# Lag attention with even and odd output parts, LayerNorm statistics on ScalarE: one change to a four-layer kernel

## The reference, cut to what matters

```python
x = x + tanh(g_xattn[0]) * autocorrelation(layernorm(x), ctx, ctx)      # the lag attention
x = x + tanh(g_ffn[0]) * moe(layernorm(x), ...)                          # its statistics are made in the stage above it

def autocorrelation(Q, K, V):            # K = V = ctx; each column on its own, L = 256 rows
    corr = ifft(fft(q) * conj(fft(k))).real
    w, idx = top_k(corr, 11); w = softmax(w)
    out = sum_i w_i * v[min(idx_i + pos, L - 1)]
```

## Time and profile before

| | |
|---|---|
| median of 3 runs | 1355.69 us (1354.49 to 1355.74) |
| profiled execution | 1356.5 us, of which 1354.8 us from the first to the last instruction (the span) |
| granted TensorE clock, mean | 0.971 |
| busy share of the span | PE 92%, DVE 58%, ACT 38%, POOL 42% |
| lag attention | 0 to 422.6 us: PE 363.6, DVE 341.8, ACT 190.0, POOL 286.9 us busy |
| the three other layers | 422.6 to 1354.8 us |

### The profile page before, as it was taken

One profiled execution on the slowest core, in us unless ns is written; L12 is line 12 of the kernel. 1 busy time (PEld: TensorE's weight loads), 2 busy tenths in 40 slices (PEclk: granted clock), 3 DMA queues, 4 the chain that ended last, 5 costly groups with the idle time before them and its releaser, 6 DMA issues. The chain is left out here.

```text
span 1354.8 us, 20940 instructions
## 1 busy us (share of the span) xinstructions
PE 1239.7 (92%) x6442; PEld 846.7 (62%) x6442; DVE 783.7 (58%) x2026; ACT 513.5 (38%) x939; POOL 573.0 (42%) x931
## 2 busy tenths in 40 slices
PE   4799999999878999999999998999999999968886
PEld 2354544445435954458888786988888898635443
DVE  3889999998963680015433333444554443369885
ACT  2555545454423400023322222232222322168894
POOL 5667877777642001013221222523212231068884
PEclk8999999999988899999999999999999999879998
DMA  5211212302004502227778874535333331131111
GB/s 197 92 64 32 93 62 96 138 31 109 0 1 149 224 1 84 70 85 246 265 240 283 273 233 161 187 94 128 114 103 124 96 101 54 62 70 47 62 62 78
DMA packets 52481, 156.25 MB, mean 115 GB/s; under 512 B 5952, under 2 KB 16192, under 8 KB 52288
## 3 DMA queue, kind: packets, MB, share of 16 engines
q1 hardware_dynamic: 39152, 113.46, 23.6%
q0 software_dynamic: 13264, 41.95, 10.8%
HBM read 112.93 MB, written 45.61 MB: 117 GB/s over the span
## 5 line engine op out<-in xcount | busy, mean ns | idle before, releaser
L1210 PEld LDWEIGHTS ex_bank<-ex_xT,ex_gu 128*112 128x112 f32 x1248 | 140.4, 177 | 24.3 <-issue 23.3
L1210 PE MATMUL ex_bank<-ex_xT,ex_gu 128*112 128x128 f32 x1248 | 143.6, 273 | 2.0 <-issue 1.0
L44 PE MATMUL xa_bank<-fT_high,M_hi 128*128 128x256 f32 x512 | 144.0, 281 | 0.0
L46 PE MATMUL xa_bank<-fT_high,M_lo 128*128 128x256 f32 x512 | 143.0, 279 | 0.0
L45 PE MATMUL xa_bank<-fT_low,M_hi 128*128 128x256 f32 x512 | 142.9, 279 | 0.0
L52 PE MATMUL la_bank<-la_osum,la_tab 128*128 128x512 f32 x256 | 120.8, 617 | 24.1 <-POOL la_osum L291 23.7
L291 POOL TENSOR_TENSOR la_osum<-la_oprod 128x512 f32<-128x512 f32 x64 | 80.1, 1273 | 73.7 <-DVE la_oprod L479 73.7
L1074 POOL TENSOR_TENSOR ex_small<-listed,ex_small 128x1 int32<-128x1 int32 x42 | 15.4, 368 | 223.7 <-DVE Wk L1152 223.5
L52 PEld LDWEIGHTS la_bank<-la_osum,la_tab 128*128 128x128 f32 x256 | 47.7, 196 | 86.4 <-issue 48.6
L44 PEld LDWEIGHTS xa_bank<-fT_high,M_hi 128*128 128x128 f32 x512 | 96.7, 189 | 0.3
L46 PEld LDWEIGHTS xa_bank<-fT_high,M_lo 128*128 128x128 f32 x512 | 96.7, 189 | 0.0
(11 more groups left out here) (284 smaller groups left out, 2853.4 us busy)
## 6 DMA issues: line engine op xcount, KB each, us to landing
produced<-Wk SPq DMA_DIRECT2D x39, 512.0 KB
ex_gu<-in_gate_up SPq DMA_DIRECT2D x16, 896.0 KB
X<-in_x SPq DMA_DIRECT2D x8, 1024.0 KB, 7.4
la_v_raw<-in_ctx SPq DMA_DIRECT2D x16, 512.0 KB, 4.0
produced<-la_zeros SPq DMA_DIRECT2D x16, 512.0 KB, 4.7
normal<-rt_xn SPq DMA_DIRECT2D x16, 512.0 KB, 5.4
fT<-in_ctx_T SPq DMA_DIRECT2D x8, 1024.0 KB, 5.7
xa_f<-in_ctx SPq DMA_DIRECT2D x8, 1024.0 KB, 4.8
```

Of the source, the lines that this page charges most:

```text
L44: pe.matmul(out, a[0], b[0], start=first, stop=False)
L46: return pe.matmul(out, a[1], b[0], start=False, stop=last)
L1210: m = pe.matmul(bank[half][0:INTER, 0:P], gu[:, slot, at:at + INTER], xT[:, k, :], start=(k == 0), stop=(k == KD - 1))
```

## The change

- **Even and odd part.** The positions are now taken as half-integers about the middle, at which the cosine kinds are even and the sine kinds odd. Kinds 0 and 3 together give one part, kinds 1 and 2 the other (`KINDS`). Row tile 0 is the sum of the parts and row tile 1 their difference, so a part is two products instead of four with each of two tables, and `add` adds each part to both row tiles (the odd one to row tile 1 with the negated gate `less_tg`). Additions: four of 512 columns a unit instead of two. Lags are counted from 0 to 255 and not in half steps: the fold of the weights leaves lag 0 and lag 128 apart (one copy more in each `w_halves`), and two more products go into the lag spectra (`last_t(2)`, `sign_t`).
- **LayerNorm statistics on ScalarE.** For `first_ln` of batches 3 to 7 and `running_ln` of batches 0 to 6. `running_ln`'s sum comes from the accumulator of the additions of the odd part; `first_ln`'s from an ACT pass. Then the squares of x less its mean, summed by an ACT pass (1024 columns, result thrown away in bf16), and the chain on POOL from there. `first_ln` of batches 0 to 2 stays on DVE.
- **Six places.** `statistic` puts one row tile's pass at each of three places of a step (after exponent 0, after exponent 1, after the second evacuation of v spectra), six in two units. What has nothing to do is a no-op with its semaphore.
- The loop is shorter by one pair (`Fori(2, B - 2)`), written out instead.
- `last_positions`, which took the last unit's output kind by kind, is gone: the last unit goes like the others.

```diff
-    rows_bank = [bank[4], bank[1]]
+    KINDS = (0, 3, 1, 2)
+    part_bank = [bank[4], bank[1]]
...
-            with eng.Fori(1, B - 2) as b:
+            with eng.Fori(2, B - 2) as b:
...
 def w_halves(u, g):
-                a, b = wt[:, two, 0:P], wt[:, two, P:L]
-                pool.tensor_tensor(w_less[:, two, :], a, b, ALU.subtract).then_inc(s["w_fold"], 1)
+                a, b = wt[:, two, 1:P], wt[:, two, P + 1:L]
+                pool.tensor_tensor(w_less[:, two, 1:P], a, b, ALU.subtract).then_inc(s["w_fold"], 1)
+                pool.tensor_copy(w_less[:, two, 0:1], wt[:, two, P:P + 1]).then_inc(s["w_fold"], 1)
                 pool.tensor_tensor(a, a, b, ALU.add).then_inc(s["w_fold"], 1)
...
 # POOL's step
+                if now and now[2] == 1 and summed_by_act(now[1]):
+                    pool.wait_ge(s["stat"], STATS * now[1] + 5)
+                    norm.on_pool_from_squares(pool, now[1] + 2)
+                if before2 and before2[2] == 0 and not (fixed(before2[1]) and before2[1] < 1):
+                    pool.wait_ge(s["stat"], STATS * (before2[1] + 1) + 1)
+                    scales_after.on_pool_from_squares(pool, before2[1] - 1)
+                if before and before[2] == 1 and not (fixed(before[1]) and before[1] == B - 1):
+                    at_least(pool, s["added1"], 2 * before[0] + 2)
+                    scales_after.means_on_pool(pool, before[1])
...
 # ACT
+            act.activation(less_tg[:], tg[:], ACT.Copy, scale=-1.0).then_inc(s["less_gate"], 1)
+            def statistic(before2, now, place):
+                pair, odd = (now[1], now[2]) if now else (before2[1] + 1, before2[2])
+                i = 3 * odd + place
+                at_least(act, s["stat"], STATS * pair + i)
+                def ahead():
+                    act.activation(stat_spare[:, i:i + 1], no_first[:], ACT.Copy)
+                def squares(scales, b, j):
+                    act.activation(junk[:], rows(b, j), ACT.Square, bias=scales.less_mean[:, j:j + 1],
+                                   accum_out=scales.squares[:, j:j + 1]).then_inc(s["stat"], 1)
+                def sum_of(b, j):
+                    act.activation(junk[:], rows(b, j), ACT.Identity, accum_out=norm.sums[:, 0, 0, j:j + 1]).then_inc(s["stat"], 1)
...
                 if now:
                     exponent(now[0], 0)
+                statistic(before2, now, 0)
+                if now:
                     exponent(now[0], 1)
+                statistic(before2, now, 1)
+                if now:
                     share(now[0], 0)
...
                 if after:
                     spectra(after[0], True)
+                statistic(before2, now, 2)
                 if now:
                     share(now[0], 2)
...
 # DVE
-            def add(u, b, h, j):
-                at_least(dve, s["out_pe"], 2 * u + j + 1)
+            def add(u, b, h, part):
+                at_least(dve, s["out_pe"], 2 * u + part + 1)
+                if part:
+                    at_least(dve, s["added0"], 2 * u + 2)
+                if part and h == 0:
+                    at_least(dve, scales_after.mean_ready, b)
+                for j in range(2):
+                    total = scales_after.sums[:, bass.ds(b % 2, 1), h, j:j + 1].rearrange("p o i -> p (o i)") if part else None
+                    xs = X[:, bass.ds(2 * b + j, 1), halfsl(h)]
+                    factor = less_tg if part and j else tg
+                    dve.scalar_tensor_tensor(out=xs, in0=part_bank[part][:].rearrange("p (a c) -> p a c", a=1), scalar=factor[:, 0:1], in1=xs,
+                                             op0=ALU.mult, op1=ALU.add, accum_out=total).then_inc(s[f"added{part}"], 1)
...
-                if before2 and before2[2] == 1 and not (isinstance(before2[1], int) and before2[1] == B - 1):
-                    scales_after.variance(dve, X, before2[1])
-                if due is not None:
+                if due is not None and fixed(due) and due <= 2:
                     dve.wait_ge(x_in, 16 * (due + 1))
                     norm.variance(dve, X, due)
...
 # PE
-                full_product(pe, bank[4][:], lags_t(0), more)
-                full_product(pe, bank[5][:], lags_t(1), less).then_inc(s["wspec"], 1)
+                full_product(pe, bank[4][:], lags_t(0), more, True, False)
+                full_product(pe, bank[4][:], last_t(2), less, False, True)
+                full_product(pe, bank[5][:], lags_t(1), less, True, False)
+                full_product(pe, bank[5][:], sign_t, more, False, True).then_inc(s["wspec"], 1)
             def positions(u, j):
-                at_least(pe, s["osums"], 4 * u + 4)
-                for i in range(4):
-                    m = full_product(pe, rows_bank[j][:], pos_t(i, j), osum[:, i, :], i == 0, i == 3)
-                m.then_inc(s["out_pe"], 1)
+                if j == 0:
+                    at_least(pe, s["oprods"], 8 * u + 6)
+                at_least(pe, s["osums"], 4 * u + 2 * j + 2)
+                full_product(pe, part_bank[j][:], pos_t(KINDS[2 * j]), osum[:, 2 * j, :], True, False)
+                full_product(pe, part_bank[j][:], pos_t(KINDS[2 * j + 1]), osum[:, 2 * j + 1, :], False, True).then_inc(s["out_pe"], 1)
...
 # BatchScale
+    def means_on_pool(self, pool, b):
+        now = self.sums[:, bass.ds(b % 2, 1), :, :].rearrange("p o h j -> p (o h) j")
+        pool.tensor_tensor(self.var, now[:, 0, :], now[:, 1, :], ALU.add).then_inc(self.summed, 1)
+        pool.wait_ge(self.summed, b + 1)
+        pool.tensor_tensor(self.less_mean, self.var, self.less_part, ALU.mult).then_inc(self.mean_ready, 1)
+    def on_pool_from_squares(self, pool, b):
+        # var = squares / D + eps, then the same chain of ten [128, 2] operations as on_pool
```

More of the change, by code:

```diff
@@ L76, in fourier_tables @@
     rows[:, 1, 0] = np.sin(np.pi * middle[:, 0])
[L77 removed]
+    last = np.zeros((3, P, P))
     last[0, 0, 0] = L
     last[1, 0] = -2 * rows[:, 2].sum(0)
[L80 to L82 removed]
+    last[2, 0] = sign
+    lags = kinds(p)
+    lags[:, 1, 0] = 0
+    lags[0, 1, 0] = 1
+    lags[0, 3] = -sign
+    found = np.concatenate([P + np.arange(P), (P - np.arange(P)) % P])[None, :]
     angle = 2 * np.pi * p * found / L
@@ L163, in lag_t, with pos_t @@
             return table(LAG_AT + kind * L, L)
-        def pos_t(kind, j):
-            return table(POS_AT + (2 * kind + j) * P, P)
+        def pos_t(kind):
+            return table(POS_AT + kind * P, P)
+        sign_t = table(SIGN_AT, P)
         names = """gw_in tab_in tab_rest gate_in Wq_in zeroed filled consts dchain
@@ L196, in one @@
                 step(on, due)
-            for u in range(-2, 2):
+            for u in range(-2, 4):
                 one(u, u // 2, u % 2)
-            with eng.Fori(1, B - 2) as b:
+            with eng.Fori(2, B - 2) as b:
                 one(2 * b, b, 0)
@@ L244, in _, with fixed, summed_by_act @@
             sp.wait_ge(s["gw_in"], 16)
+        junk, stat_spare = sb("junk", [P, D], BF16), sb("stat_spare", [P, 6])
+        STATS = 6
+        def fixed(b):
+            return isinstance(b, int)
+        def summed_by_act(b):
+            return not fixed(b) or 1 <= b < B - 2
         @block.gpsimd
@@ L475, in o_products @@
                 pairs = (((0, 4), (2, 5)), ((2, 4), (1, 5)), ((3, 6), (4, 7)), ((4, 6), (3, 7)))
-                for i, two in enumerate(pairs):
+                for i in range(4):
+                    two = pairs[KINDS[i]]
                     at_least(dve, s["osums"], 4 * u + (i - 1 if i >= 2 else 0))
@@ L506, in step @@
                 if now:
-                    lags(now[0], last_rows, products)
+                    lags(now[0], odd_part, products)
                 else:
-                    last_rows()
+                    odd_part()
                     products()
@@ L628, in __init__ @@
         self.mv = sb("mv", [P, 2, 2])
-        small = sb("small", [P, 12, 2])
-        self.var, self.root, self.power, self.eps, self.step, self.spare, self.less, self.half, self.more, self.now, self.other, self.one = (small[:, i, :] for i in range(12))
+        small = sb("small", [P, 16, 2])
+        (self.var, self.root, self.power, self.eps, self.step, self.spare, self.less, self.half, self.more, self.now, self.other, self.one,
+         self.part, self.less_part, self.less_mean, self.squares) = (small[:, i, :] for i in range(16))
+        self.sums = sb("sums", [P, 2, 2, 2])
         self.scale, self.shift = (sb(n, [P, TILES]) for n in ("scale", "shift"))
     def signal_with(self, sem):
-        self.chain, self.var_ready, self.set, self.links, self.taken, self.ready = (
-            sem(f"{self.tag}_{n}") for n in ("chain", "var_ready", "set", "links", "taken", "ready"))
+        self.chain, self.var_ready, self.set, self.links, self.taken, self.ready, self.summed, self.mean_ready = (
+            sem(f"{self.tag}_{n}") for n in ("chain", "var_ready", "set", "links", "taken", "ready", "summed", "mean_ready"))
     def prepare(self, pool):
```

(19 more changed lines are left out.)

91 lines of the change are left out of this document (51 added, 40 removed).

## The result

| | before | after |
|---|---|---|
| median | 1355.72 us (1354.49 to 1356.04, 4 runs) | 1360.66 us (1359.63 to 1362.94, 4 runs) |
| ratio of after to before | | 1.004, 95% interval 1.0023 to 1.0058 |
| span of the profiled execution | 1354.8 us | 1357.9 us |
| 14 steps, from product to product | 329.84 us, 58.37 to 388.21 | 334.83 us, 59.15 to 393.98 |

What follows compares the result with a forecast made beforehand. It took a chain over four engines to bound the step's first half and VectorE the second. Span 1354.8 + 2.2 + 6.5 (clock) + 0.2 = 1363.7 us, forecast as 1364 by the median, range 1351 to 1373.

Steps and rivals of the forecast that it cites:

- Statistics off DVE, worth 0: First half of the step: removing 2.78 us of LN statistics from VectorE gains 0, since the chain covers them.
- ACT's passes, cost 0: Three statistics passes a step on ScalarE, 1.4 us each, fit its idle time, also ahead of share 2; cost 0.
- Copies, +0.30 for W: Two GpSimd copies a step, 0.15 us each, move W, the weight folds' end, from T+12.96 to T+13.26 (T: step start).
- The meeting at block 0: VectorE's masked share of block 0 meets GpSimd's third fold; VectorE goes on at W+3.94, or W+4.04 by the skill's rule.
- Second half, 6.82 us: From block 0's masked share to the next step: VectorE alone, two additions instead of one, 5.97 to 6.82 us.
- Sum of the chain, +3.5 us: The 14 steps: 8 at 24.0, five at 23.6, the last at 23.2, 333.3 us against 329.84.
- The clock, +6.5 us: A 2.2 us TensorE hole ahead of the correlation lowers its clock, +1.3 us a step in 5 of 13 steps.
- Start-up +0.7, tail −2.0, the other layers +0.2: Outside the 14 steps: start-up 0.3 to 1, tail −3.6 to 0, two more memsets in each later LayerNorm.
- no fall of the clock: Rival: TensorE's clock does not fall at the hole ahead of the correlation; 1358 us, 30%.
- DVE wins the race for block 3: Rival: VectorE's masked share precedes GpSimd's fold, 0.6 us a step gained, 1350 us; 19% together with free copy and accumulator.
- the move of the statistics gains outright: Rival: LN off VectorE gains 2.78 − 1.5 us a step, −18 us, 1338 us; 1%.
- ACT as the bound: Rival: ScalarE passes of 2.2 us or more at place 2 push exponent 3, 0.5 to 1 us a step, 1375 us; 8%.

Runs made afterwards that it cites:

- experiment 2: Before, without the BN_STATS of LayerNorms in the loop and written-out steps (stale statistics); ratio 1.0100, 14 steps 328.54 us.
- 11: experiment 8's kernel with the BN_STATS left out as in experiment 2 (stale statistics); ratio 1.0004, 14 steps 320.88 us.
- experiment 5: After, with LN statistics back on VectorE and no passes, accumulators or squares on ScalarE; ratio 1.0115, 14 steps 344.85 us.
- 12: After with the waits of experiment 1, experiment 3 and experiment 4, LN statistics back on VectorE; ratio 0.9997, 14 steps 328.63 us.
- 6: After, with ScalarE's six statistics passes cut from 1024 to 8 columns; ratio 1.0040, 14 steps 333.70 us.
- experiment 10: After, with every statistics pass of ScalarE done twice; ratio 1.0045, 14 steps 333.80 us.
- 7: After, with the three waits of experiment 1, experiment 3 and experiment 4 together; ratio 0.9935, 14 steps 319.65 us.
- experiment 1: After, with part 0 of the positions waiting for all four GpSimd sums, splitting TensorE's hole; ratio 1.0025, 14 steps 331.26 us.
- experiment 4: After, with the first weight fold's addition on GpSimd waiting for the masked share of block 3; ratio 1.0028, 14 steps 334.06 us.
- experiment 3: After, with GpSimd's two q folds waiting for the masked share of the next unit's block 0; ratio 0.9980, 14 steps 325.88 us.
- experiment 8: Before, with the two GpSimd waits of experiment 3 and experiment 4, no even and odd part; ratio 0.9933, 14 steps 320.73 us.
- 9: Kernel 7 with one copy for both weight folds, behind the last; ratio 0.9910, 14 steps 317.98 us.

## Why the prediction was right, and which of its sizes were off

The forecast of a slower kernel was right, and so were the place of the loss and its mechanisms; two of the sizes were too large, the clock's above all. The sum, step by step:

- **Statistics off DVE, worth 0.** Right: experiments 2 and 11. What the trace of before could not show is that the same move is worth 9 us and more once the even and odd part is in (5, 12).
- **ACT's passes, cost 0.** Right (6, 10). A pass is 1.15 us and its accumulator read 0.20, forecast 1.4 together; 0.71 us remain ahead of share 2. The Trainium skill, page "ScalarE: Activation LUTs", section "Rules for kernel authors", would have left these sums on VectorE. That VectorE is the faster engine for them agrees with the trace (three passes of 1.05 to 1.15 us and their reads a step on ACT, 2.8 us on DVE), but beside the second addition DVE had no room and ACT had: by experiments 7 and 12 following the rule costs 9 us there.
- **Copies, +0.30 for W.** Half of it in the loop: W is T+13.10 there, not 13.26 (in the steps written out it is some T+13.2). The second copy costs its spacing, 0.14; the first cost nothing, since POOL's folds begin at T+8.96 instead of T+9.07, so the addition that blocks DVE starts at T+9.78, where it was T+9.76.
- **PE.** Correlation at T+9.06 for 9.2, transposes at T+13.28 for 13.4. Right.
- **The meeting at block 0.** DVE goes on at W+3.94, as in the start-up, so at T+17.04 for 17.20. The Trainium skill, page "SBUF — State Buffer", section "Who interferes with whom": of two such instructions the first goes and the other waits for all of it. The trace agrees in kind: the share asked at 220.12 us, when its exponent ended (219.61 and 0.51), in the middle of L284 (from 219.55), and took 0.43 us more than alone. Its end by that rule was put at W+4.04, 0.10 too late.
- **Second half, 6.82 us.** 6.93 in one step of the pair and 6.63 in the other. The two additions follow each other by 0.68 us (223.76, 224.44), so the accumulator output costs nothing (0.08 forecast). The wait and the register work ahead of them leave 0.60 us of idle time in one step of the pair, where before has 0.32, and 0.30 in the other, where before has 0.26: 0.16 on average, for 0.1.
- **Sum of the chain, +3.5 us.** Measured where no clock falls (experiment 1): 331.26 against 329.84, +1.4. The loop steps are 23.85 for 24.0, the written-out ones 23.5 for 23.6. The first copy is the term that was too large, with 0.15 us in each loop step.
- **The clock, +6.5 us.** The term that was most wrong, and in size alone: 3 falls of 1.2 us, 3.6 us, where 5 of 1.3 were taken. A fall does what was said: transposes 1.1 us later, the share past the fourth fold. How many there would be was a guess. No run settles it, and with another number of falls the result would have come out nearer to the forecast or to its rival; that part is luck.
- **Start-up +0.7, tail −2.0, the other layers +0.2.** Measured +0.78, in single executions: the first of these products lies at 57.0 to 58.4 us in the four kernels of the old form and at 58.2 to 59.2 in the ten of the new one. The tail is −1.9 (from the last of these products to the last addition 32.4 us instead of 34.3). Of it −2.7 lies behind the last unit's product, as forecast, and +0.75 ahead of it. The 0.7 that the lag spectra were to give back is right as a sum and not as told: TensorE's clock is at its full level over them (12 records in 5.4 us, where before has 8 in 3.6), so they cost 1.8, and 1.05 had been gained ahead of them. The other layers are 0.7 shorter; that was not traced, and is within the scatter of single executions (before runs from 1349.26 to 1357.84 us in one group).

The last positions that answer to the earlier trace rows:

```profile
419.48 5.43 PE L52 MATMUL la_bank<-la_osum,la_tab 128*128 128x512 f32 x8 [4.11 <-DVE la_oprod L559]
```

0.78 + 1.42 + 3.57 − 1.92 − 0.73 = 3.1 us of span, for 8.9 forecast. The medians stand nearer to the forecast (4.9 us for 8.3) because before's profiled execution lies above its median and after's below its own.

Of the rivals, "no fall of the clock" (1358) would have been after less 3.6, and the result lies between it and the forecast. "DVE wins the race for block 3" was missed by 0.14 us: the addition begins at 213.78, DVE asks at 213.92. Its price of 0.6 us a step was too high: experiment 4 gives 0.4 in the steps with no fall. That the move of the statistics gains outright (1338) is out by experiment 2, and ACT as the bound by experiment 10.

## What to carry to other kernels

Where the engine in question waits in one half of the step and works in the other, moving work off it pays only in the half where it works: here 25 us of covered work were worth nothing, and one addition of 0.67 us in the other half cost itself in every step. Whether work is covered changes with what stands beside it: the same statistics were worth 9 us and more after the second addition came in. Look for two engines that block each other over SBUF at the same place of every step; one wait that turns their order (a "who goes first" that costs the loser nothing) was worth 5 us in experiment 3 (325.88 against 331.26, neither with a fall) and 9 in experiment 8, to which the restructuring adds nothing. And when work leaves TensorE, look at the hole that it leaves in one piece: with a later start that splits it, no clock fell in four kernels, and with the hole whole it fell in five of six.

## What the runs showed of the hardware that was not expected

- A hole of the same length lets the granted clock fall in some steps and not in others. With the positions early there were 0, 2, 2, 3, 5 and 7 falls in 14 steps (experiments 3, 6, 10, after, 5, 4), with them late none in any of four kernels (1, 7, 9, 12). All 19 falls stand in steps with 1.86 to 3.11 us of idle PE ahead of the correlation by the records. Of the other 65 steps with early positions none of the 37 with a shorter hole has a fall, which takes in every step of experiment 3, and 28 with a hole as long (1.87 to 3.10) have none either. So every fall here had a long hole ahead of it, and most of the long holes had no fall behind them. In experiment 4 the two kinds of step differ by it: the correlations at 91.11, 139.00, 186.97, 234.96, 282.97, 330.53 and 377.94 us follow 1.89 to 2.24 us and are slow, those between follow 1.66 or less and are not. What picks among the long ones stays open: no run changes the hole or the step's length alone.
- In these kernels a fall costs only where the chain through PE is what the others wait for: 1.1 to 1.2 us a step in after, next to nothing in experiment 5, where DVE is the bound (its steps 5, 8 and 12, with a fall, are as long as 7, 10 and 13, without, to 0.02 us).
- A kernel with a shorter chain can so be no faster: experiment 4 lost to the clock what it won from POOL. The same edit beside those of 1 and 3 took 6.2 us off the 14 steps (325.88 in experiment 3, 319.65 in 7, neither with a fall).
- ACT's accumulator read is an instruction of its own, 0.19 to 0.20 us behind each pass, and the next one begins 0.1 us after it starts.
- Where DVE waits behind a fold of POOL and goes next, POOL's following fold shows the delay: 1.46 us for L285 instead of 1.27.
